# Splitting the attention scores around one projection group in steps 33 to 45 of a two-layer cross-attention kernel

## The chip, the cores and the metric

The kernel runs on one core of a Trainium2 chip. Its time is device microseconds (us) of that core, the median of three runs. The engines are TensorE (PE, with its weight loads shown apart as PEld), VectorE (DVE), ScalarE (ACT), GpSimd (POOL) and SyncE (SP), which here only issues DMAs. Each of them works through its own instructions in the order written, and they wait for each other by counting semaphores.

## The reference

There are 32 sequences of 64 tokens with 128 features, a context of the same shape, and a key mask. They pass a decoder layer (self-attention, cross-attention, feed-forward) and then a second cross-attention with rotary positions. The kernel treats this as three attention layers of 16 heads with 64 channels each; the change lies in the third:

```python
q = rope((x @ Wq).reshape(B, Sq, 16, 64)) / sqrt(64)      # x: output of the first layer
k = rope((ctx @ Wk).reshape(B, Skv, 16, 64))
v = (ctx @ Wv).reshape(B, Skv, 16, 64)
scores = einsum('bhqd,bhkd->bhqk', q, k)
attn = softmax(where(mask, scores, -1e9))
out = einsum('bhqk,bhkd->bqhd', attn, v).reshape(B, Sq, 1024) @ Wo
y = layernorm(x + out)
```

All of it is float32; a projection is three matmuls, on inputs and weights split into a high and a low part (L524 to L526).

## The kernel before

**Units and steps.** Two sequences (128 tokens) make a unit. 16 units times 3 attention layers are 48 pieces of work, numbered 0 to 47; a software pipeline of steps -2 to 49 overlaps them. Unit 32 is the first of the third layer. In step u TensorE does the scores of unit u, the transposes of the probabilities of an earlier unit, the weighted values and the output projection of unit u-2, the values of unit u, and half of the projections for the two units that come next: queries in an even step, keys in an odd one. The feed-forward part of the second layer still runs in steps 33 and 35 (every odd step up to there).

**Scores.** `scores(u)` writes the mask of all heads into ps_a (four PSUM banks, L553, 8 matmuls) and adds the products of queries and keys (L561, 64 matmuls of 32-row tiles, which the trace shows as 128). It starts when the exponentials of the unit before have been read out of ps_a and when the rotated keys are there. One semaphore, `scored`, is raised once, by the last of them.

**Fills and the ring.** Everything else that TensorE writes goes through a ring of four PSUM banks, ps_p0 to ps_p3. A *fill* is the filling of one bank (for the weighted values two). `fills(u)` lists the fills of a step in order, with the engine that empties each; fill number n uses bank n mod 4 and first waits until fill n-4 has been emptied (`bank_free`). The names in the list are:

- PP: transposes of the probabilities of unit u-2 (L660), copied out by ScalarE (L771).
- Qr or Kr, 0 to 3 (here r0 to r3): one quarter of the queries or keys (6 matmuls, L524 to L526), multiplied with the rotary tables by VectorE (L924), added by GpSimd (L1178). The tables' products have two buffers.
- O, two fills: weighted values (L601), copied out by ScalarE (L759).
- V, two fills: values (L649 to L651), copied by ScalarE (L769).
- FT (L700), F1, F2 (L716): feed-forward; FT transposes its input, split into high (ScalarE L764) and low part (VectorE L914).
- Y: output projection (L694), added to the residual by VectorE (L947).
- T: transposes of the inputs of the next queries (L639), at the end of an odd step, split into a high part by ScalarE (L762) and a low part by VectorE (L911). Query group r0 of the next step reads both.

**The order on the other engines.** VectorE's own list (`vector_order`) for such a step is: late feed-forward pieces, the maximum over the scores (L997), FT, r0 to r3, half of the normalisation of the unit before (L1042), the sums (L1027), Y and its statistics, F2, T. ScalarE goes through the fills in the order of `fills(u)`, with the first eight exponentials (L805) ahead of O and the other eight ahead of V; eight heads are scaled (L821) after V or F1, ahead of T.

Of the kernel before, what the change touches and what calls it, by code (L numbers as in the profile page):

```python
# [13 lines left out]
B, S, E = 32, 64, 128  # L14
H, D = 16, 64
PAIRS = H // 2
UNITS = B // 2
# [15 lines left out]
def projected(u):  # L33
    g = u // 2 + 1
    return g if g < N // 2 else None


def ffn_chunk(u):
    g = (u - 5) // 2
    return g if u % 2 and UNITS // 2 <= g < UNITS else None  # L40


def attends(u):
    return 0 <= u < N


def turns(u):
    return 0 <= u - 1 < N


def finishes(u):
    return 0 <= u - 2 < N


def rotary(u):
    return projected(u) is not None and projected(u) * 2 // UNITS == 2
# [7 lines left out]
def heads_in_ring(u):  # L64

    return finishes(u) and u >= 2 * UNITS
# [18 lines left out]
def by_head(u):  # L85

    return attends(u) and rotary(u)


def defers(u):  # L90

    return by_head(u) and u > 2 * UNITS - 1


def turned_by(u):

    return "AA" if by_head(u) or u >= N - 2 else "DD"
# [17 lines left out]
def fills(u):  # L115

    heads = [("O", b, "D" if u >= N and b else "A") for b in range(2)] if heads_in_ring(u) else []
    turn_in = [("T", 0, "AD")] if u % 2 == 0 and UNITS <= 2 * (u // 2 + 1) and projected(u) is not None and not by_head(u) else []
    values = [("V", j, "A") for j in range(2)] if attends(u) else []
    probabilities = [("P", j, turned_by(u)[j]) for j in range(2)] if turns(u) and not defers(u) else []  # L120
    deferred = [("PP", j, "A") for j in range(2)] if defers(u - 1) else []
    result = [("Y", 0, "D")] if finishes(u) else []
    project = []
    if projected(u) is not None:
        name = "K" if u % 2 else "Q"
        for j in range(4):
            project.append((name + "r", j, "D") if rotary(u) else (name, j, ("AAAD" if u == FIRST else "ADAD" if u < 0 else "AAAA")[j]))
    next_in = [("T", 0, "AD")] if u % 2 and by_head(u + 1) else []
    if by_head(u):

        ffn = [("FT", 0, "AD")], [("F1", 0, "A"), ("F1", 1, "A")], [("F2", 0, "D")]
        into, inside, outof = ffn if ffn_chunk(u) is not None else ([], [], [])
        return deferred + into + project[:2] + heads + project[2:] + values + inside + result + outof + probabilities + next_in
    if ffn_chunk(u) is not None:
        return [("FT", 0, "AD")] + values + probabilities + [("F1", 0, "A"), ("F1", 1, "A")] + project + [("F2", 0, "D")] \
            + result + next_in
    if u == N - 2:

        return deferred + values + heads + probabilities + result
    if u % 2:  # L140
        return heads + values + probabilities + project + result
    return deferred + heads + turn_in + values + probabilities + project[:3] + result + project[3:]
# [128 lines left out]
def build(nc, a, out):  # L271
    ctx = ExitStack()
    with ctx:
        def sb(name, shape, dt=F32):
            return ctx.enter_context(nc.sbuf_tensor(name, shape, dt))
# [4 lines left out]
        def sem(name):  # L280
            return ctx.enter_context(nc.semaphore(name))
# [43 lines left out]
        qT = sb("qT", [128, 2, PAIRS, CT])  # L325
        kT = sb("kT", [128, 2, PAIRS, CT])
# [37 lines left out]
        ps_a = ctx.enter_context(nc.psum_tensor("ps_a", [128, 4, 512], F32))  # L364
# [25 lines left out]
        scored = sem("scored")  # L390
# [69 lines left out]
        def head_at(u):  # L460
            return [n for n, _, _ in fills(u)].index("O")
# [58 lines left out]
        def _(pe):  # L520
            mm = nc.tensor.matmul
# [6 lines left out]
            def scores(u):  # L528
                par, v, layer = u // 2 % 2, u % 2, u // UNITS

                if by_head(u - 1):
                    pe.wait_ge(exped, EXPED.before(u))
                elif SHIFTED.before(u):
                    pe.wait_ge(shifted, SHIFTED.before(u))

                if layer == 2:

                    pe.wait_ge(rotated, ROTATED.at(u - 1 - v, "Kr", 3, v))
                elif v == 0:
                    out_of_bank(u - 1, "K", 2)  # L540
                    out_of_bank(u - 1, "K", 3)
                if layer == 2:
                    if u == 2 * UNITS:
                        pe.wait_ge(setup_dve, FOLD)

                        pe.wait_ge(headed, HEADED.before(u))


                    for i in range(4):
                        for b in range(2):  # L550
                            of = slice(32 * i, 32 * i + 32)
                            m = mask[of, 1, u % UNITS, b:b + 1, :]
                            mm(ps_a[64 * b:64 * b + 64, i ^ b, 0:256], fold[of, :], m.broadcast_to([32, 4, S]),  # L553
                               start=True, stop=False, skip_group_check=True)
                    for quad in range(H // 4):
                        for half in range(2):
                            for i in range(4):
                                for b in range(2):
                                    t = (2 * v + b) * S
                                    of = slice(32 * i, 32 * i + 32)  # L560
                                    last = mm(ps_a[64 * b:64 * b + 64, i ^ b, 64 * quad:64 * quad + 64],  # L561
                                              qT[of, par, 2 * quad + half, t:t + S], kT[of, par, 2 * quad + half, t:t + S],
                                              start=False, stop=half == 1, skip_group_check=True)
                    last.then_inc(scored, 1)
                    return


                for h in range(2):
                    for b in range(2):
                        of = slice(64 * h, 64 * h + 64)  # L570
                        m = mask[of, 0 if layer == 0 else 1, u % UNITS, b:b + 1, :]
                        mm(ps_a[64 * b:64 * b + 64, h ^ b, :], eye_bf[of, of], m.broadcast_to([64, 8, S]),  # L572
                           start=True, stop=False, skip_group_check=True)
                for p in range(PAIRS):
                    for h in range(2):
                        for b in range(2):
                            t = (2 * v + b) * S
                            of = slice(64 * h, 64 * h + 64)
                            last = mm(ps_a[64 * b:64 * b + 64, h ^ b, 64 * p:64 * p + 64],  # L579
                                      qT[of, par, p, t:t + S], kT[of, par, p, t:t + S],  # L580
                                      start=False, stop=True, skip_group_check=True)
                last.then_inc(scored, 1)

            def weight_values(u):
                w, last = u - 2, None
# [24 lines left out]
            def out_of_bank(u, name, j):  # L610

                who = {(n, k): w for n, k, w in fills(u)}[name, j]
                if "A" in who:
                    pe.wait_ge(act_emptied, EMPTY_A.at(u, name, j))
                if "D" in who:
                    pe.wait_ge(dve_emptied, EMPTY_D.at(u, name, j))
# [103 lines left out]
            def bias_of_values():  # L720

                for layer in range(2):
                    pe.wait_ge(multiplied, MULTIPLIED * (layer + 1))
                    mm(ps_a[:, 2 + layer, 0:E], valid[:, 2, 0:1].broadcast_to([128, 128]), products(layer)[:, 0, :],
                       start=True, stop=True).then_inc(bvwo_done, 1)
# [8 lines left out]
            for u in range(FIRST, END):  # L734
                if u in (0, READY):
                    pe.wait_ge(setup_dve, MASKED if u else FIRST_MASKED)
                if attends(u) and u != N - 1:
                    scores(u)
                if u == 2:
                    pe.wait_ge(bvwo_read, 2)  # L740
                if finishes(u) and not heads_in_ring(u):
                    weight_values(u)
                for at, (name, j, _) in enumerate(fills(u)):
                    if (u, name, j) == (N - 2, "P", 0):
                        scores(N - 1)
                    if (name, j) == ("O", 0):
                        weight_values(u)
                    elif name != "O":
                        fill(u, at, name, j)
                if u == 1:  # L750
                    bias_of_values()

# [595 lines left out]
```

## Time and profile before

| | us |
|---|---|
| median of 3 runs | 519.58 (519.25 to 519.75) |
| the profiled execution | 519.46 |
| its span in the trace | 517.6 |
| PE busy | 500.0 (97%) |
| DVE busy | 433.2 (84%) |
| ACT busy | 361.2 (70%) |
| POOL busy | 312.6 (60%) |

The span runs from the first to the last instruction that the trace records; 1.86 us of the profiled execution lie around it. Busy times of PE are modelled from pipelined matmuls: consecutive matmuls overlap in the list, and the distance between two starts is the better measure of what one costs. Steps 33 to 45 lie between 348.2 and 488.5 us; the first mask matmul (L553) of each step marks its start.

### The profile page before, as it was taken

The page shows a single profiled execution, that of the slowest core. Times are in us where ns is not written, and L with a number is a line of the kernel's source. Part 1 is how long each engine was busy: PE and PEld are TensorE (multiplying, and loading weights), DVE is VectorE, ACT ScalarE, POOL GpSimd, SP SyncE. Part 2 cuts the span into 40 slices and gives each one's busy share as a digit, 9 for nine tenths or more (in the row PEclk, how much of TensorE's full clock was granted, in tenths as well). Part 3 has the DMA queues.
Part 4 walks back from the last instruction along what each step waited for, and adds up shares of the span by engine and source line. Part 5 has one row for each costly group of instructions (what it writes and reads, how often), then busy time and mean ns, then how long its engine had stood idle before and what let it go on. Part 6 is the DMA issues. An engine that isn't in the chain of part 4 may idle for free.

```text
span 517.6 us, 23719 instructions
## 1 busy us (share of the span) xinstructions
PE 500.0 (97%) x10308; PEld 465.1 (90%) x10308; DVE 433.2 (84%) x761; ACT 361.2 (70%) x987; POOL 312.6 (60%) x611
## 2 busy tenths in 40 slices
PE   8889999999999999999999999999999999999985
PEld 7789999999999999999999997889999999999975
DVE  4988999978899878877778788998988888889883
ACT  6575765765866756756567685778687887888761
POOL 2836445536438545434646337888777887888735
PEclk9999999999999999999999999999999999999999
DMA  8910000000022010000000000000000000000000
GB/s 241 357 62 15 3 11 14 3 13 13 3 48 79 3 44 3 3 3 1 4 1 3 3 3 1 3 3 3 4 8 10 15 8 10 8 14 8 10 9 22
DMA packets 10039, 13.80 MB, mean 27 GB/s; under 512 B 848, under 2 KB 7376, under 8 KB 9936
## 3 DMA queue, kind: packets, MB, share of 16 engines
q1 hardware_dynamic: 9936, 12.28, 7.6%
q8 instruction: 82, 1.34, 1.1%
q14 instruction: 21, 0.17, 0.1%
HBM read 11.23 MB, written 1.05 MB: 24 GB/s over the span
## 4 chain that ended last, share of the span: by engine, by line
PE 78%; ACT 13%; DVE 4%; issue 2%; POOL 1%; DMA 1%; POOLq 0%; SPq 0%; DVEq 0%
PE ps_p L694 13%; PE ps_p L524 8%; PE ps_p L526 7%; PE ps_p L525 7%; PE ps_p L660 7%; ACT kT L777 6%; PE ps_a L579 5%; PE ps_a L601 5%; PE ps_p L649 5%; PE ps_a L561 4%; PE ps_p L651 4%; PE ps_p L650 4%; PE ps_p L601 3%; PE ps_p L716 2%; ACT probs L815 2%; PE ps_a L572 2%
## 5 line engine op out<-in xcount | busy, mean ns | idle before, releaser
L1217 POOL TENSOR_TENSOR small<-mv,epsilon 128x1 f32<-128x1 f32 x48 | 9.6, 199 | 147.5 <-DVE mv L953 147.5
L694 PE MATMUL ps_p<-wo,headsT 128*128 128x128 f32 x768 | 93.9, 275 | 1.6 <-DVE headsT L932 0.9
L694 PEld LDWEIGHTS ps_p<-wo,headsT 128*128 128x128 f32 x768 | 90.4, 192 | 3.5 <-DVE turn L924 1.1
L769 ACT ACTIVATE vv<-ps_p 128x512 f32<-128x512 f32 x96 | 57.1, 616 | 49.4 <-PE ps_p L651 46.1
L924 DVE TENSOR_TENSOR turn<-ps_p,rope 128x1024 f32<-128x1024 f32 x64 | 76.1, 1221 | 11.8 <-PE ps_p L526 10.2
L524 PE MATMUL ps_p<-xT_hi,wq_hi 128*128 128x256 f32 x192 | 58.8, 306 | 0.6 <-DVE wq_lo L1053 0.5
L805 ACT ACTIVATE probs<-ps_a,top 128x64 f32<-128x64 f32 x256 | 56.0, 353 | 4.3 <-DVE top L997 3.4
L1027 DVE TENSOR_REDUCE total<-probs 128x16 f32<-128x1024 f32 x48 | 58.1, 1210 | 0.2
L777 ACT ACTIVATE qT<-ps_p,columns 128x256 f32<-128x256 f32 x126 | 49.4, 496 | 10.2 <-PE ps_p L526 10.2
L1001 DVE TENSOR_REDUCE top<-ps_a 128x8 f32<-128x512 f32 x64 | 41.0, 683 | 18.1 <-PE ps_a L579 17.9
L526 PE MATMUL ps_p<-xT_hi,wq_lo 128*128 128x256 f32 x192 | 54.3, 283 | 0.3 <-issue 0.3
L525 PE MATMUL ps_p<-xT_lo,wq_hi 128*128 128x256 f32 x192 | 54.3, 283 | 0.0
L660 PE MATMUL ps_p<-eye,probs 128*128 128x128 f32 x384 | 50.9, 275 | 1.1 <-DVE probs L1042 1.1
L660 PEld LDWEIGHTS ps_p<-eye,probs 128*128 128x128 f32 x384 | 43.5, 141 | 6.5 <-ACT vv L769 1.3
L1178 POOL TENSOR_TENSOR qT<-turn 128x512 f32<-128x512 f32 x32 | 43.7, 1387 | 7.7 <-DVE turn L924 7.7
L1178 POOL TENSOR_TENSOR kT<-turn 128x512 f32<-128x512 f32 (+1 forms) x40 | 45.5, 1162 | 4.4 <-DVE turn L924 4.4
L777 ACT ACTIVATE kT<-ps_p,columns 128x256 f32<-128x256 f32 x124 | 47.5, 522 | 0.8 <-PE ps_p L526 0.8
L1042 DVE TENSOR_TENSOR probs<-probs,rinv 128x512 f32<-128x512 f32 x62 | 42.3, 720 | 1.0
L930 DVE COPY probsT<-ps_p 128x512 f32<-128x512 f32 x58 | 37.2, 682 | 6.1 <-PE ps_p L660 6.0
L524 PE MATMUL ps_p<-cT_hi,wk_hi 128*128 128x256 f32 x128 | 38.6, 302 | 0.1
L524 PEld LDWEIGHTS ps_p<-xT_hi,wq_hi 128*128 128x128 f32 x192 | 37.1, 193 | 1.7 <-issue 0.7
L771 ACT ACTIVATE probsT<-ps_p 128x512 f32<-128x512 f32 x38 | 20.6, 596 | 25.7 <-PE ps_p L660 25.7
(145 smaller groups left out, 1396.8 us busy)
## 6 DMA issues: line engine op xcount, KB each, us to landing
out<-y_out SPq DMA_DIRECT2D x16, 64.0 KB, 1.5
raw<-in_x_turned SPq DMA_DIRECT2D x1, 768.0 KB, 9.9
across<-in_across SPq DMA_DIRECT2D x1, 704.0 KB, 7.3
raw<-in_ctx_turned SPq DMA_DIRECT2D x5, 128.0 KB, 2.3
wq_raw<-in_L_xattn_sa_wq SPq DMA_DIRECT2D x2, 256.0 KB, 3.8
wk_raw<-in_L_xattn_sa_wk SPq DMA_DIRECT2D x1, 512.0 KB, 5.1
wv_raw<-in_L_xattn_sa_wv SPq DMA_DIRECT2D x1, 512.0 KB, 7.3
wo<-in_L_xattn_sa_wo SPq DMA_DIRECT2D x1, 512.0 KB, 8.5
```

What stands on the lines that cost most here:

```text
L524: mm(dst, w[0], x[0], start=True, stop=False)
L525: mm(dst, w[0], x[1], start=False, stop=False)
L526: return mm(dst, w[1], x[0], start=False, stop=True)
L660: last = nc.tensor.transpose(bank[:, 128 * pp:128 * pp + 128], probs[:, unit % 2, at_head:at_head + 2, :].rearrange("q h k -> q (h k)"), e ...
L694: last = mm(bank[:, 0:E], headsT[:, p, :, :].rearrange("r b q -> r (b q)"), wo[:, layer % 2, p, :], start=(p == 0), stop=(p == PAIRS - 1))
L769: ins = nc.scalar.activation(vv[:, u % 2, j, :, :].rearrange("k p d -> k (p d)"), bank[:, :], ACT.Copy)
L777: ins = nc.scalar.activation(to[:, g % 2, p, :], bank[:, CT * k:CT * k + CT], ACT.Identity, bias=bias[:, g * CU // UNITS, p:p + 1])
L805: ins = nc.scalar.activation(probs[:, u % 2, n, :], ps_a[:, bank, 64 * k:64 * k + 64], ACT.Exp, bias=top[:, at:at + 1], scale=scale)
L924: ins = V.tensor_tensor(turn[:, j % 2, :, :].rearrange("d a (h b t) -> d a h b t", h=2, t=S), bank[:, None, :].broadcast_to([128, 2, 512]) ...
L1027: V.tensor_reduce(total[:, :], probs[:, u % 2, :, :], AX_X, ALU.add).then_inc(dve_step, 1)
L1042: V.tensor_tensor(p, p, factor[:, u % 2, 8 * j:8 * j + 8, None].broadcast_to([128, 8, S]), ALU.mult)\
L1178: G.tensor_tensor(to[:, projected(u) % 2, 2 * j:2 * j + 2, of], *[t[:, :, of] for t in turned(j)], ALU.add).then_inc(rotated, 1)
```

## The change

In steps 33 to 45 TensorE's work is put in another order. `scores` now issues the masks and the first two of the four groups of score matmuls; then comes the first projection group r0 (in steps 33 and 35 the fill FT ahead of it), then the other two groups of score matmuls with the signal `scored`, and then the fills PP, r1, O, r2, r3 and so on. Before, the order was scores, PP, (FT,) r0, r1, O, r2, r3. Which matmuls there are does not change, nor does VectorE's list. ScalarE's list has FT ahead of PP in steps 33 and 35. Since the fills stand in another order, they sit in other banks of the ring.

```diff
+def scores_apart(u):
+
+    return by_head(u) and u > 2 * UNITS
...
-        return deferred + into + project[:2] + heads + project[2:] + values + inside + result + outof + probabilities + next_in
+        first, project = (project[:1], project[1:]) if scores_apart(u) else ([], project)
+        k = 2 - len(first)
+        return into + first + deferred + project[:k] + heads + project[k:] + values + inside + result + outof + probabilities + next_in
...
-                    for quad in range(H // 4):
...
-                    last.then_inc(scored, 1)
+                    score_quads(u, range(2))
+                    if not scores_apart(u):
+                        score_quads(u, range(2, 4))
                     return
...
+            def score_quads(u, quads):
+
+                par, v = u // 2 % 2, u % 2
+                for quad in quads:
+                    for half in range(2):
+                        for i in range(4):
+                            for b in range(2):
+                                t = (2 * v + b) * S
+                                of = slice(32 * i, 32 * i + 32)
+                                last = mm(ps_a[64 * b:64 * b + 64, i ^ b, 64 * quad:64 * quad + 64],
+                                          qT[of, par, 2 * quad + half, t:t + S], kT[of, par, 2 * quad + half, t:t + S],
+                                          start=False, stop=half == 1, skip_group_check=True)
+                if quad == H // 4 - 1:
+                    last.then_inc(scored, 1)
...
+                    if name[1:] == "r" and j == 0 and scores_apart(u):
+                        score_quads(u, range(2, 4))
```

TensorE's rows from the start of step 36 to its first projection group or second score half, before the change (ps_p0 to ps_p3 are the ring's banks, and brackets name the semaphores that a row waits for):

```order
L553 MATMUL ps_a<-mask,fold 64x256 [waits rotated,exped]
L553 MATMUL ps_a<-mask,fold 64x256 x7
L561 MATMUL ps_a<-kT,qT 64x64 x64
L660 MATMUL ps_p2<-eye,probs 128x128 [waits normed,act_emptied]
L660 MATMUL ps_p2<-eye,probs 128x128 x3
L660 MATMUL ps_p3<-eye,probs 128x128 [waits normed_rest,dve_emptied]
L660 MATMUL ps_p3<-eye,probs 128x128 x3
L524 MATMUL ps_p0<-xT_hi,wq_hi 128x256 [waits dve_emptied,act_emptied]
L525 MATMUL ps_p0<-xT_lo,wq_hi 128x256
L526 MATMUL ps_p0<-xT_hi,wq_lo 128x256
```

The same place of the changed kernel (its line numbers are other ones: L560 is the mask, L593 a score, L675 a transpose, L531 to L533 a projection):

```order
L560 MATMUL ps_a<-mask,fold 64x256 [waits rotated,exped]
L560 MATMUL ps_a<-mask,fold 64x256 x7
L593 MATMUL ps_a<-kT,qT 64x64 x32
L531 MATMUL ps_p2<-xT_hi,wq_hi 128x256 [waits dve_emptied,act_emptied]
L532 MATMUL ps_p2<-xT_lo,wq_hi 128x256
L533 MATMUL ps_p2<-xT_hi,wq_lo 128x256
L531 MATMUL ps_p2<-xT_hi,wq_hi 128x256
L532 MATMUL ps_p2<-xT_lo,wq_hi 128x256
L533 MATMUL ps_p2<-xT_hi,wq_lo 128x256
L593 MATMUL ps_a<-kT,qT 64x64 x32
L675 MATMUL ps_p3<-eye,probs 128x128 [waits normed,dve_emptied]
L675 MATMUL ps_p3<-eye,probs 128x128 x3
```

The r0 group has moved from behind eight transposes to the middle of the scores and from bank ps_p0 to ps_p2.

TensorE a little later in step 36, from the last r1 matmuls into O, before:

```order
L524 MATMUL ps_p1<-xT_hi,wq_hi 128x256
L525 MATMUL ps_p1<-xT_lo,wq_hi 128x256
L526 MATMUL ps_p1<-xT_hi,wq_lo 128x256
L601 MATMUL ps_p2<-probsT,vv 64x64 [waits act_emptied]
L601 MATMUL ps_p3<-probsT,vv 64x64
```

and in the changed kernel (L616 is O):

```order
L531 MATMUL ps_p1<-xT_hi,wq_hi 128x256
L532 MATMUL ps_p1<-xT_lo,wq_hi 128x256
L533 MATMUL ps_p1<-xT_hi,wq_lo 128x256
L616 MATMUL ps_p2<-probsT,vv 64x64 [waits dve_emptied,act_emptied]
L616 MATMUL ps_p3<-probsT,vv 64x64
```

O's first bank was last written by a PP fill before the change and is last written by r0 after it, and the first O matmul has gained a wait for VectorE.

## Rows read from the trace of the kernel before

**Rows 1.** The page: busy us, share of the span, instructions.
```profile
PE 500.0 (97%) x10308; PEld 465.1 (90%) x10308; DVE 433.2 (84%) x761; ACT 361.2 (70%) x987; POOL 312.6 (60%) x611
```

**Rows 2.** Windows, step 37 and a gap: length, busy (instructions), PEclk, DMA share, GB/s.
```profile
397.17:407.42 10.25, 10.25 (x257) 9.55 (x256) 9.35 (x14) 8.52 (x32) 8.38 (x13) 1.00 0.04 10
...
495.20:496.70 1.50, 0.01 (x2) 0.01 (x2) 0.27 (x2) 0.65 (x2) 0.00 (x0) 1.00 0.00 0
```

**Rows 3.** Timeline, step 37: start, length, engine, line, instruction, count [idle before].
```profile
397.17 0.32 PE L553 MATMUL ps_a<-mask,fold 32*64 32x256 bf16 x8
...
398.77 1.09 PE L660 MATMUL ps_p<-eye,probs 128*128 128x128 f32 x8
...
399.07 1.22 DVE L997 TENSOR_REDUCE top<-ps_a 128x16 f32<-128x1024 f32 x1
...
399.62 0.37 PE L524 MATMUL ps_p<-cT_hi,wk_hi 128*128 128x256 f32 x1
...
399.83 0.28 PE L525 MATMUL ps_p<-cT_lo,wk_hi 128*128 128x256 f32 x1
...
400.43 0.28 PE L524 MATMUL ps_p<-cT_hi,wk_hi 128*128 128x256 f32 x1
...
400.70 2.35 DVE L924 TENSOR_TENSOR turn<-ps_p,rope 128x1024 f32<-128x1024 f32 x2 [0.42 <-PE ps_p L526]
...
401.03 0.28 PE L526 MATMUL ps_p<-cT_hi,wk_lo 128*128 128x256 f32 x1
401.24 1.16 PE L601 MATMUL ps_p<-probsT,vv 64*64 64x64 f32 x64
```

**Rows 4.** Timeline, from the exponentials of step 37 to O of step 38.
```profile
403.43 1.75 ACT L805 ACTIVATE probs<-ps_a,top 128x64 f32<-128x64 f32 x8
...
407.42 0.32 PE L553 MATMUL ps_a<-mask,fold 32*64 32x256 bf16 x8
...
407.93 0.38 ACT L762 ACTIVATE xT_hi<-ps_p 128x256 fp32r<-128x256 f32 x1
...
408.60 0.39 DVE L911 TENSOR_TENSOR xT_lo<-ps_p,xT_hi 128x256 fp32r<-128x256 f32 x1
...
409.14 1.22 DVE L997 TENSOR_REDUCE top<-ps_a 128x16 f32<-128x1024 f32 x1 [0.15 <-PE ps_a L561]
...
411.49 1.16 PE L601 MATMUL ps_p<-probsT,vv 64*64 64x64 f32 x64
```

**Rows 5.** Timeline, step 33, with the feed-forward fill FT.
```profile
348.23 0.32 PE L553 MATMUL ps_a<-mask,fold 32*64 32x256 bf16 x8
...
350.76 0.38 PE L700 MATMUL ps_p<-eye,x 128*128 128x128 f32 x2
...
350.90 0.37 PE L524 MATMUL ps_p<-cT_hi,wk_hi 128*128 128x256 f32 x1
...
351.92 0.42 DVE L914 TENSOR_TENSOR x2T_lo<-ps_p,x2T_hi 128x256 fp32r<-128x256 f32 x1 [0.76 <-ACT x2T_hi L764]
...
352.26 2.34 DVE L924 TENSOR_TENSOR turn<-ps_p,rope 128x1024 f32<-128x1024 f32 x2
...
352.51 1.16 PE L601 MATMUL ps_p<-probsT,vv 64*64 64x64 f32 x64
...
354.66 0.39 PE L524 MATMUL ps_p<-cT_hi,wk_hi 128*128 128x256 f32 x1
```

**Rows 6.** Timeline, step 34.
```profile
362.15 0.32 PE L553 MATMUL ps_a<-mask,fold 32*64 32x256 bf16 x8
...
362.67 0.42 DVE L911 TENSOR_TENSOR xT_lo<-ps_p,xT_hi 128x256 fp32r<-128x256 f32 x1 [0.21 <-ACT xT_hi L762]
...
365.38 0.39 PE L526 MATMUL ps_p<-xT_hi,wq_lo 128*128 128x256 f32 x1 [0.29 <-issue]
...
366.78 1.16 PE L601 MATMUL ps_p<-probsT,vv 64*64 64x64 f32 x64
```

**Rows 7.** Timeline, a projection matmul near the kernel's start.
```profile
6.50 0.42 PE L525 MATMUL ps_p<-xT_lo,wq_hi 128*128 128x256 f32 x1
```

More of the change, by code:

```diff
@@ L554, in scores @@
                                start=True, stop=False, skip_group_check=True)
-                    for quad in range(H // 4):
[L556 to L563, printed above, removed]
-                    last.then_inc(scored, 1)
+                    score_quads(u, range(2))
+                    if not scores_apart(u):
+                        score_quads(u, range(2, 4))
                     return
```

## The prediction, made before the changed kernel ran

> **What bounds the kernel now.** I read the page's busy line first, then the windows, then the timeline of single steps. TensorE is busy for 500.0 of 517.6 us [rows 1], and in step 37 for 10.25 of 10.25 us at granted clock 1.00 [rows 2]: there is no idle time of TensorE in which a new wait could hide. VectorE and ScalarE have 0.9 and 1.7 us to spare in that step [rows 2]. So whatever holds TensorE up inside a step goes onto the end, and whatever only moves work about on the others does not, unless TensorE comes to wait for it. The question for each edit is which wait TensorE meets, and when it is released.
>
> I measure inside a step from its first mask matmul, t0, and need where O starts, because from O on nothing changes its order: the next step starts 407.42 - 401.24 = 6.18 us after O in step 37 [rows 3, 4], and the exponentials, copies, rotations and sums behind it follow from O and the r2 that comes after it. O starts at +4.07 in step 37 (401.24 - 397.17) and in step 38 (411.49 - 407.42) [rows 3, 4].
>
> **The change part by part.**
>
> *r0 ahead of the signal `scored`.* Masks and scores take 398.77 - 397.17 = 1.60 us [rows 3]. The masks are at most 0.32 of it, and as their ends overlap with the scores I take 0.24; a half of the scores is then 0.68 us. A projection group takes 400.43 - 399.62 = 0.81 us, where five spaces of 0.12 (400.43 - 399.83) and a first one of 0.21 show that changing the kind of matmul costs 0.09; from the last projection matmul to O it is 0.21 again (401.03 to 401.24), another 0.09 [rows 3]. The group in the middle therefore delays `scored` by 0.81 + 0.09 = 0.90 us. This switch was not between these two kinds in the trace; the bounds are 0 and 0.2 each, and I take 0.09, the value of both neighbours.
>
> *VectorE behind it.* VectorE's list is unchanged: maximum first, then r0. Where VectorE was free, the maximum started at +1.72 (409.14 - 407.42) [rows 4]; in step 37 it was late by itself, at +1.90 [rows 3], which the new delay covers. Now it starts at 1.72 + 0.90 = +2.62 and ends at +3.84 (1.22 long). r0's rotation follows at once, and takes 2.35 / 2 = 1.18 [rows 3]: it ends at +5.04. Before, it waited 0.42 us for its matmuls after the maximum [rows 3]; that idle time is gone, and it is the only thing won.
>
> *The bank that O wants.* With four banks in a ring, O's first fill is the fourth after r0 in the new order (r0, PP, PP, r1, O), so it waits for r0's rotation. Before, it followed a PP fill, emptied by ScalarE well in time. TensorE would be ready for O at +4.25 (4.07 and the two added switches), but the bank is free at +5.04. In step 33 the matmul that waited for a rotation (r3, 354.66) began 0.06 us after that rotation ended (352.26 + 2.34 = 354.60) [rows 5]. So O starts at 5.04 + 0.06 = +5.10, where it was +4.07: 1.03 us lost in each step, the switches included. r1's rotation follows r0's and is over at +6.2; r2's can come only after O (about 1.1 us) and r2's matmuls (0.81), at +7.0 or later, so the two buffers of the tables' products and GpSimd behind them are not late. Behind TensorE's waiting instruction stand r2, r3, V, Y and the next scores, the whole rest of the step. The exponentials' second half ended 403.43 + 1.75 = 405.18, 3.94 us after O [rows 3, 4], and the next scores come 6.18 after it, so this older wait keeps 2.2 us of slack.
>
> *r0 in an even step needs T.* Query group r0 reads the inputs that T turned at the end of the odd step before. Before the change r0 came at about +2.45, and the low part was ready at 408.60 + 0.39 - 407.42 = +1.57 [rows 4]. Now r0 is wanted at 0.24 + 0.68 = +0.92. T's split comes at the same distance from the step's start as before, because ScalarE reaches it behind work that hangs on O (407.93) and VectorE behind the statistics of Y (408.60). So r0 starts at 1.57 + 0.06 = +1.63, which is 0.71 us late, all of it ahead of `scored`: maximum at +3.3, r0's rotation done at +5.73, O at +5.79 or 0.7 more than in an odd step: 1.72 us lost in steps 38, 40, 42 and 44. In steps 34 and 36, behind a feed-forward step, the split was ready at 362.67 + 0.42 - 362.15 = +0.94 [rows 6], so r0 is 0.09 late there and the loss is 1.1 us.
>
> *Steps 33 and 35, with FT.* FT takes 350.90 - 350.76 = 0.14 of TensorE, also ahead of `scored` now. VectorE: maximum from 1.72 + 0.90 + 0.14 = +2.76 to +3.98, FT's low part to +4.3 (0.34 from 351.92 to 352.26), rotation of r0 to +5.5, O at +5.55; before it was 352.51 - 348.23 = +4.28 [rows 5]. r1 now waits for FT's bank, but that ends sooner than r0's rotation. Against the 1.27 stands the wait of r3 for the rotation of r1 that goes: from O at 352.51, with 1.1 for O and 0.8 for r2, it should have started at about 354.4 and did at 354.66, 0.2 late [rows 5]. I take 0.2 in both steps, so about 1.07 each.
>
> *The gap in step 34.* TensorE stood still for nothing that the trace names at 365.38, before O, and O came at +4.63 (366.78 - 362.15) instead of about +4.1 [rows 6]. Such a pause belongs to a place in the instruction stream; the new order puts the transposes there, which have 0.8 us of slack before O. So step 34 loses only 5.19 - 4.63, some 0.6 us. If the gap falls ahead of `scored` instead, 0.5 more.
>
> *Sum:* steps 37, 39, 41, 43, 45: 5 x 1.03 = 5.15. Steps 38, 40, 42, 44: 4 x 1.72 = 6.88. Steps 33 and 35: 2.15. Steps 34 and 36: 0.6 + 1.1 = 1.7. Together 15.9 us, against the profiled execution's own 519.46 (span 517.6 and 1.86 around it): 535.3. The median of the runs is 0.12 higher, so 535.5 us. Nothing after step 45 takes it back: step 46 starts from O of step 45 like any other. With both switches at 0 the sum is 2.3 less (13 x 0.18), with 0.2 each 2.9 more.
>
> **A rule weighed.** TensorE will stand still for 0.8 us in the middle of every step, and in every second step for 0.7 us more. In the trace a pause of 1.5 us in the scores of unit 47 (495.2 to 496.7, TensorE busy for 0.01) left the granted clock at 1.00, the 2.4 GHz level [rows 2].
>
> The Trainium skill says otherwise for a pattern like this: "TensorE: Matmul & The Clock Gate", section "A second HAM failure mode: psum-queue depth-cycling", tells of a kernel that cycled through PSUM banks, paused a little between groups of matmuls, and had its clock swing between the two levels. By the trace the term is 0; by that rule the time would be that of the rival on the clock below. The trace of before has no such regular pauses, so it neither agrees nor disagrees.
>
> **The rivals.**
>
> *T does not bind (the smaller loss).* If T's split is done by +0.9, every step loses the 1.03 to 1.1 of the bank wait alone: 15.9 - 4 x 0.69 = 13.1, or 532.7 us. Against it: ScalarE's copy starts at +0.51 and ends at +0.89 in step 38, and VectorE only takes the low part up at +1.18 [rows 4]; what stands ahead of both hangs on O.
>
> *A second chain turns late (the larger loss).* ScalarE's exponentials follow the maximum, the copies of O follow them, and the second exponentials follow those; then V and the scaling. If one of these comes to hold the next scores, 0.3 to 0.6 us more per step, 4 to 8 us: 539 to 543. Against it: 2.2 us of slack as worked out above.
>
> *The clock falls.* At the lower level a projection matmul took 0.42 us at the kernel's start against 0.28 [rows 7, 3], with the work of a step near double. If the clock were low for a fifth of the 13 steps, that is some 2.5 x 10 = 25 us more: 560.
>
> *Not slower: the bank is free in time.* VectorE waits 0.42 us for r0's matmuls today [rows 3], so whoever takes VectorE for the late engine sees it gain: r0 is there when the maximum ends, r3's waits in steps 33 and 35 vanish, and TensorE pays nothing as long as r0's rotation ends by +4.25 in a step. Then the time is 519.2 (519.6 less 0.4). The deciding point is that rotation: by my sum it ends at +5.04. It would have to start before the maximum, or maximum and rotation would have to be 0.8 us shorter together than their rows. The list has the maximum first, so I give it little.
>
> **How the numbers follow.** Forecast as summed 0.73, T not binding 0.12, a second chain 0.07, the clock 0.03, not slower 0.05. The forecast's own spread comes from the switches (-2.3, +2.9) and the gaps (0.5): 533.2 to 538.9. The range of 531.5 to 540 takes in the case in which T does not bind and the near end of the larger loss. Under 0.2% (1.0 us) nothing can be told from no change. All but the last case are slower, 0.95; of its 0.05 I put 0.03 on the same and 0.02 on faster.
>
> **What would show it.** In the profile after: TensorE idle before O (L616), released by VectorE's rotation, about 0.8 us in each of 13 steps; idle before the first projection matmul of even steps from 38 on, released by VectorE's xT_lo, about 0.7 us; the rotation right behind the maximum with no idle time; steps 37 to 45 of 11.3 us where odd (5.10 + 6.18) and 11.8 where even (no T at the end). The chain of waits should show L924 and L997 with a share each. It is wrong if O starts before +4.5, if the mask of the next step comes later than 6.3 us after O, or if the granted clock leaves 1.00.

## The result, and the profile after

The changed kernel takes 540.02 us (median of 5 runs, 539.03 to 541.28) against 519.59 us before (5 runs): slower, ratio 1.039, 95% interval 1.0371 to 1.041. The forecast was 535.5 us with a range of 531.5 to 540: the direction and the mechanism held, the size was 4.5 us short, and the median stands at the upper end of the range. The profiled execution took 541.28 us and its span is 539.4 us.

The page of the changed kernel, first part, answers to [rows 1]:

```profile
PE 506.7 (94%) x10308; PEld 469.0 (87%) x10308; DVE 431.6 (80%) x761; ACT 360.4 (67%) x987; POOL 311.3 (58%) x611
```

The same instructions, but TensorE stands still for 32.7 us of the span where it did for 17.6. What it waited for is in the view of waits, for TensorE from 345 to 520 us (waiting line, releaser: us in total, times, longest):

```profile
PE ps_p L616 <- DVE turn L941: 10.5, 13, 0.9
PE ps_p L531 <- DVE xT_lo L928: 2.9, 4, 0.7
PE ps_a L593 <- issue: 1.6, 1, 1.6
PE ps_p L531 <- ACT probsT L788: 1.4, 2, 0.7
```

Thirteen waits of O (L616) for the rotation, four of the first projection matmul for T's low part: the counts are those of the forecast. The third row is the pause in unit 47's scores, which the kernel before had too [rows 2]. The fourth is named wrongly, as shown below.

Windows after (length, busy (instructions) of PE, PEld, DVE, ACT, POOL, PEclk, DMA share, GB/s): from the first mask matmul of step 33 to that of step 46, step 37, step 38, from unit 47's scores to the end, and a piece of that:

```profile
348.86:508.66 159.80, 144.74 (x3375) 132.23 (x3375) 121.20 (x172) 113.76 (x408) 112.11 (x161) 1.00 0.03 8
402.31:413.89 11.58, 10.68 (x259) 9.74 (x258) 9.37 (x14) 8.52 (x32) 8.36 (x13) 1.00 0.03 9
413.89:426.01 12.12, 10.48 (x256) 9.55 (x256) 8.73 (x13) 8.34 (x31) 8.01 (x12) 1.00 0.03 8
...
513.76:539.40 25.64, 18.85 (x429) 17.37 (x422) 13.68 (x28) 9.78 (x18) 9.94 (x23) 0.92 0.06 16
518.12:521.53 3.41, 3.41 (x18) 3.33 (x16) 1.76 (x3) 2.08 (x4) 0.00 (x0) 0.50 0.03 5
```

The first and fourth stretch before the change:

```profile
348.23:488.48 140.25, 139.63 (x3375) 130.02 (x3375) 122.74 (x172) 114.16 (x408) 112.28 (x161) 1.00 0.03 9
...
493.56:517.50 23.94, 17.22 (x429) 15.79 (x422) 13.72 (x28) 9.78 (x18) 9.96 (x23) 0.96 0.06 17
```

So 159.80 - 140.25 = 19.55 us lie in the thirteen changed steps. Of the 21.8 us between the two profiled executions, 0.6 lie ahead of step 33, where no instruction is changed, and 1.6 behind the start of step 46, where TensorE ran for 3.41 us at half the clock (last row). By what is on record it does not depend on the change: the traces of e2, e3 and e6 have such a stretch too (e3 a second one, at about 17 to 23 us), those of before, e1, e4, e5, e7, e8 and e10 do not, though e4 and e7 make TensorE wait at O as this kernel does. Executions of either kernel with a mean clock of 0.995 or 0.996 are the longer ones: 541.2 and 541.3 us against 539.0 to 540.0 for the changed kernel, and in the rounds of e1 to e4 520.8 to 521.3 against 518.8 to 519.7 for the kernel before. Below, experiments are compared by the time from step 33's to step 46's first mask matmul, called *the stretch*, 140.25 us before and 159.80 after.

The timeline of step 37 after, answering to [rows 3] (start, length, engine, line, instruction [idle before]):

```profile
402.31 0.32 PE L560 MATMUL ps_a<-mask,fold 32*64 32x256 bf16 x8
...
403.27 0.40 PE L531 MATMUL ps_p<-cT_hi,wk_hi 128*128 128x256 f32 x1
...
403.98 0.28 PE L533 MATMUL ps_p<-cT_hi,wk_lo 128*128 128x256 f32 x1
...
404.19 0.92 PE L593 MATMUL ps_a<-kT,qT 32*64 32x64 f32 x64
...
405.03 1.09 PE L675 MATMUL ps_p<-eye,probs 128*128 128x128 f32 x8
405.14 1.23 DVE L1014 TENSOR_REDUCE top<-ps_a 128x16 f32<-128x1024 f32 x1 [0.79 <-PE ps_a L593]
...
406.28 2.35 DVE L941 TENSOR_TENSOR turn<-ps_p,rope 128x1024 f32<-128x1024 f32 x2
...
407.58 2.53 POOL L1195 TENSOR_TENSOR kT<-turn 128x512 f32<-128x512 f32 x2 [0.64 <-DVE turn L941]
...
407.76 1.16 PE L616 MATMUL ps_p<-probsT,vv 64*64 64x64 f32 x64 [0.90 <-DVE turn L941]
```

The reader is to see the chain: r0's last matmul ends at 404.26, but VectorE stands idle for 0.79 us, because its next instruction is the maximum and the scores end at 405.0. The rotation follows at 406.28, and O starts at 407.76, 5.45 us after the step's start where it was 4.07.

Step 38, answering to [rows 4]:

```profile
414.40 0.41 ACT L779 ACTIVATE xT_hi<-ps_p 128x256 fp32r<-128x256 f32 x1
...
415.12 0.39 DVE L928 TENSOR_TENSOR xT_lo<-ps_p,xT_hi 128x256 fp32r<-128x256 f32 x1
415.65 0.36 PE L531 MATMUL ps_p<-xT_hi,wq_hi 128*128 128x256 f32 x1 [0.74 <-DVE xT_lo L928]
...
420.11 1.10 PE L616 MATMUL ps_p<-probsT,vv 64*64 64x64 f32 x60 [0.90 <-DVE turn L941]
```

r0 waits for T's low part and starts 1.76 us into the step (415.65 - 413.89) instead of 0.96, and O comes at 6.22.

Step 33, answering to [rows 5]:

```profile
353.00 0.41 DVE L931 TENSOR_TENSOR x2T_lo<-ps_p,x2T_hi 128x256 fp32r<-128x256 f32 x1
353.34 2.52 DVE L941 TENSOR_TENSOR turn<-ps_p,rope 128x1024 f32<-128x1024 f32 x2
...
353.57 0.36 PE L531 MATMUL ps_p<-cT_hi,wk_hi 128*128 128x256 f32 x1 [0.72 <-ACT probsT L788]
...
354.81 1.16 PE L616 MATMUL ps_p<-probsT,vv 64*64 64x64 f32 x64 [0.28 <-DVE turn L941]
```

r1 wants FT's bank, which VectorE empties at 353.41, and starts 0.16 later. The profile puts this wait down to ScalarE's probsT, which r1 has nothing to do with; the program's order tells who it is (r1's bank is FT's). It shortens the wait at O to 0.28.

### The profile page after: what moved, and what is told of

It is laid out like the page before. It is cut to its first block, busy times and chain, and to the rows that moved or that the text cites. A ratio compares the mean times of both kernels' runs of the same rounds, so it can differ in the third digit from the quotient of the medians.

```text
span 539.4 us, 23721 instructions
## 1 busy us (share of the span) xinstructions
PE 506.7 (94%) x10308; PEld 469.0 (87%) x10308; DVE 431.6 (80%) x761; ACT 360.4 (67%) x987; POOL 311.3 (58%) x611
## 4 chain that ended last, share of the span: by engine, by line
PE 69%; ACT 12%; DVE 10%; issue 5%; POOL 1%; DMA 1%; SPq 0%; POOLq 0%; DVEq 0%
PE ps_p L709 12%; PE ps_p L531 7%; ACT kT L794 6%; PE ps_p L532 6%; PE ps_p L533 6%; PE ps_a L579 5%; PE ps_a L616 5%; DVE turn L941 5%; PE ps_a L593 4%; PE ps_p L664 4%; PE ps_p L675 4%; PE ps_p L616 4%; PE ps_p L666 3%; PE ps_p L665 3%; PE ps_p L731 2%
## 5 line engine op out<-in xcount | busy, mean ns | idle before, releaser
L709 PE MATMUL ps_p<-wo,headsT 128*128 128x128 f32 x768 | 95.5, 278 | 1.6 <-DVE headsT L949 0.9
L709 PEld LDWEIGHTS ps_p<-wo,headsT 128*128 128x128 f32 x768 | 92.0, 194 | 3.5 <-DVE turn L941 1.1
L531 PE MATMUL ps_p<-xT_hi,wq_hi 128*128 128x256 f32 x192 | 59.1, 308 | 3.1 <-DVE xT_lo L928 2.9
L794 ACT ACTIVATE qT<-ps_p,columns 128x256 f32<-128x256 f32 x126 | 49.3, 496 | 10.2 <-PE ps_p L533 10.2
L533 PE MATMUL ps_p<-xT_hi,wq_lo 128*128 128x256 f32 x192 | 54.1, 282 | 0.0
L675 PE MATMUL ps_p<-eye,probs 128*128 128x128 f32 x384 | 50.9, 275 | 1.0 <-DVE probs L1059 1.0
L675 PEld LDWEIGHTS ps_p<-eye,probs 128*128 128x128 f32 x384 | 43.5, 141 | 6.3 <-ACT vv L786 1.2
L531 PEld LDWEIGHTS ps_p<-xT_hi,wq_hi 128*128 128x128 f32 x192 | 37.0, 193 | 4.8 <-ACT xT_hi L779 3.4
L531 PE MATMUL ps_p<-cT_hi,wk_hi 128*128 128x256 f32 x128 | 38.8, 303 | 1.4 <-ACT probsT L788 1.4
```

The costliest lines, as they stand in the source:

```text
L531: mm(dst, w[0], x[0], start=True, stop=False)
L533: return mm(dst, w[1], x[0], start=False, stop=True)
L675: last = nc.tensor.transpose(bank[:, 128 * pp:128 * pp + 128], probs[:, unit % 2, at_head:at_head + 2, :].rearrange("q h k -> q (h k)"), e ...
L709: last = mm(bank[:, 0:E], headsT[:, p, :, :].rearrange("r b q -> r (b q)"), wo[:, layer % 2, p, :], start=(p == 0), stop=(p == PAIRS - 1))
L794: ins = nc.scalar.activation(to[:, g % 2, p, :], bank[:, CT * k:CT * k + CT], ACT.Identity, bias=bias[:, g * CU // UNITS, p:p + 1])
```

## The experiments

The theory: TensorE's waits for VectorE (O for r0's rotation behind the maximum, r0 for T) make most of the loss. The rivals: the cut itself does (TensorE's own time), or later chains do. Diffs are against the changed kernel unless said otherwise; ratios are to the kernel before in the same rounds.

**e1: r0's rotation (and FT) ahead of the maximum on VectorE.**

```diff
-        return fout + fgain + maxima + those("FT") + those("Qr", "Kr") + before ...
+        early, rest = (those("FT") + those("Qr", "Kr")[:1], those("Qr", "Kr")[1:]) if scores_apart(u) else ...
+        return fout + fgain + early + maxima + rest + before ...
```

> The changed kernel (540.0 us), but in steps 33 to 45 VectorE takes FT and the rotation of r0 ahead of the maximum over the scores. Theory A (O waits for r0's rotation, which waits behind the maximum): the wait before O is gone; what stays is 0.40 us per step of TensorE's own (measured in the trace after: the scores end 2.72 us after the step's start with r0's 0.72 in them, where 1.60 + 0.72 would do) and the wait for T in steps 38, 40, 42, 44 (0.81 each): 519.6 + 13 x 0.40 + 4 x 0.81 less the 1.1 of pauses and r3 waits that the change removed = about 527 us. Theory B (TensorE pays for the split itself and for the changes of the kind of matmul; the order on VectorE is only seen in passing): 538 to 540 us. Theory C (the later maximum holds the exponentials and through them the next scores): slower than 540.

Measured: 528.4 us (ratio 1.0164, 1.0139 to 1.019); the stretch is 148.66, 11.1 us shorter than after the change. Step 37 of e1 begins at 398.02:

```profile
400.08 1.23 DVE L942 TENSOR_TENSOR turn<-ps_p,rope 128x1024 f32<-128x1024 f32 x1
...
401.22 1.21 DVE L1015 TENSOR_REDUCE top<-ps_a 128x16 f32<-128x1024 f32 x1
401.44 1.09 ACT L789 ACTIVATE probsT<-ps_p 128x512 f32<-128x512 f32 x2 [2.17 <-PE ps_p L676]
...
402.62 1.16 PE L617 MATMUL ps_p<-probsT,vv 64*64 64x64 f32 x64
```

All that TensorE waited for in e1 from 345 to 515 us:

```profile
PE ps_p L532 <- DVE xT_lo L929: 3.4, 4, 0.9
PE ps_a L594 <- issue: 2.1, 1, 2.1
```

The wait at O is gone, O comes at +4.60. That is 0.13 later than the 4.07 and the cut's 0.40, some 1.7 us in thirteen steps, and so most of what e1 is above the 527 expected. By the rows, ScalarE's second copy of PP (401.44 + 1.09 = 402.53) is now the last thing O needs; no run tested that alone. The wait for T has stayed. Theory A holds, C falls, and B keeps the 0.40 per step only.

**e2: the change in odd steps alone.**

```diff
-    return by_head(u) and u > 2 * UNITS
+    return by_head(u) and u > 2 * UNITS and u % 2 == 1
```

> The change in the seven odd steps 33 to 45 alone. If each step's loss is its own (5 x 1.32, 2 x 1.34 by the trace after) and the wait for T belongs to even steps that issue r0 early: 519.6 + 9.3 = 529 us, with even steps back at 10.04 us from start to start. Rival: losses pass from one step to the next (an even step pays for the odd step before it), then even steps stay longer than 10.04 and the time is 531 to 535.

Measured: 528.3 us (ratio 1.017, 1.0141 to 1.0199), the stretch 148.59. Two mask matmuls and the O between them:

```profile
399.41 0.32 PE L560 MATMUL ps_a<-mask,fold 32*64 32x256 bf16 x8
...
404.85 1.16 PE L616 MATMUL ps_p<-probsT,vv 64*64 64x64 f32 x64 [0.91 <-DVE turn L941]
...
410.98 0.32 PE L560 MATMUL ps_a<-mask,fold 32*64 32x256 bf16 x8
```

Step 37 takes 11.57 us, as after the change (11.58), and step 38 takes 10.03, as before it (10.04). Each step pays for itself, and no wait for T is left in the trace. The odd steps' losses are those of the changed kernel, 9.3 us in seven steps; the stretch grew by only 8.34, because the pauses that the kernel before has in steps 34 and 36 are gone here. By the table below, the six even steps have the larger share of the 19.55, 10.2 us.

**e3: half the maximum.**

```diff
+                    kept = S // 2 if scores_apart(u) else S
-                                    ps_a[:, :, 0:256].rearrange("q m (f k) -> q m f k", k=S), AX_X, ALU.max,
+                                    ps_a[:, :, 0:256].rearrange("q m (f k) -> q m f k", k=S)[:, :, :, 0:kept], AX_X, ALU.max,
```

> The changed kernel, with VectorE's maximum in steps 33 to 45 taken over the first 32 of each head's 64 keys (the softmax is shifted by another number than the maximum). The instruction is about 0.54 us shorter (1024 elements against 512: 1.22 against 0.68 us in the trace). Theory A: each of the 13 steps is shorter by just that, 540 - 7 = 533 us, and the idle time before O falls from 0.9 to about 0.4. Theory B: no change, 540 us.

Measured: 534.2 us (ratio 1.0278, 1.0238 to 1.0317), the stretch 152.81, 6.99 us shorter for an expected 7. Step 37, which begins at 402.17:

```profile
405.00 0.69 DVE L1015 TENSOR_REDUCE top<-ps_a 128x16 f32<-128x512 f32 x1 [0.81 <-PE ps_a L593]
405.61 2.43 DVE L941 TENSOR_TENSOR turn<-ps_p,rope 128x1024 f32<-128x1024 f32 x2
...
407.08 1.11 PE L616 MATMUL ps_p<-probsT,vv 64*64 64x64 f32 x61 [0.37 <-DVE turn L941]
```

The maximum is 0.54 us shorter and O 0.54 us earlier (+4.91 against +5.45), one for one. The maximum is on the path in each of the thirteen steps. The median is only 5.9 us below that of the changed kernel, because three of e3's four runs have a mean clock of 0.989 to 0.995; the fourth, at 0.999, took 532.2 us against 539.0 and 539.1.

**e4: two waits ahead of O instead of four.**

```diff
-                for j in range(2):
-                    ...
-                        bank_free(u, head_at(u) + b)
+                if scores_apart(u):
+                    pe.wait_ge(act_emptied, EMPTY_A.at(u, "PP", 1))
+                    pe.wait_ge(dve_emptied, EMPTY_D.at(u, "Qr" if u % 2 == 0 else "Kr", 0))
+                else: ...
```

> The changed kernel, with the waits ahead of O's first matmul put down as two (one for ScalarE's last copy, then the one for VectorE) instead of four with VectorE's third. In the trace after, O starts 0.25 us after the end of r0's rotation where r3 in step 33 of before, with one wait, started 0.06 after. If the order and number of waits make that: 13 x 0.15 to 0.2 less, 537.5 to 538 us, and O at +5.3 instead of +5.45. If the delay belongs to how TensorE restarts after standing still, no change.

Measured: 537.7 us (ratio 1.0344, 1.0315 to 1.0373), the stretch 158.40, 1.4 us shorter. Step 37 begins at 401.48:

```profile
405.45 2.34 DVE L945 TENSOR_TENSOR turn<-ps_p,rope 128x1024 f32<-128x1024 f32 x2
...
406.81 1.16 PE L620 MATMUL ps_p<-probsT,vv 64*64 64x64 f32 x64 [0.79 <-DVE turn L945]
```

O now starts 1.36 us after the rotation does, where it was 1.48 (407.76 - 406.28): about 0.11 saved (0.79 us of waiting for 0.90), half of what was in question. The edit changed the number and the order of the waits at once, so which of the two counts is open. Of the rest, some 0.14 after the rotation's end, the same is seen at r0 in step 38 (415.65, 0.14 after 415.51). Why one wait in step 33 of before was met within 0.06 [rows 5] stays open.

**e7: T ahead of the values in steps 37, 39, 41, 43.**

```diff
-        ... project[k:] + values + inside + result + outof + probabilities + next_in
+        turned, next_in = (next_in, []) if scores_apart(u) and ffn_chunk(u) is None else ([], next_in)
+        ... project[k:] + turned + values + inside + result + outof + probabilities + next_in
```

(and T's low part right behind the rotations in VectorE's list)

> The changed kernel, but in steps 37, 39, 41 and 43 the fill T comes ahead of the values (V) on TensorE, and its copies ahead of V on ScalarE and of the normalisation on VectorE. Theory A (in steps 38, 40, 42, 44 r0 waits 0.81 us for T's low part): r0 at +0.96 instead of +1.77 there, even steps 11.3 us instead of 12.13; against that up to 0.2 us in the odd steps where Y's bank now was r3's. 537 us. Rival: r0 waits for something else there (its bank, or the rotation tables' buffer): 540 us and r0 still at +1.77.

Measured: 538.3 us (ratio 1.0376, 1.0357 to 1.0396), the stretch 158.48. The end of step 37 and the start of step 38:

```profile
412.15 0.41 DVE L930 TENSOR_TENSOR xT_lo<-ps_p,xT_hi 128x256 fp32r<-128x256 f32 x1
412.29 2.05 PE L711 MATMUL ps_p<-wo,headsT 128*128 128x128 f32 x16 [0.17 <-DVE turn L943]
414.27 0.32 PE L562 MATMUL ps_a<-mask,fold 32*64 32x256 bf16 x8
...
415.23 0.39 PE L533 MATMUL ps_p<-xT_hi,wq_hi 128*128 128x256 f32 x1
```

T's low part is ready before the step starts, r0 comes at +0.96, and the even steps take 11.35 instead of 12.13 us. The odd ones give 0.45 of that back (12.03 against 11.58), more than the 0.2 expected: Y now waits for r3's rotation (0.17 in the row); the other 0.28 came with T's new place behind r3, and what makes them was not tested. T was what r0 waited for; the repair is worth less than half of it, and the time is 538.3 us where 537 was expected.

**e5: the cut around PP instead of around r0.** The fills stand as in the kernel before, and the second half of the scores follows the second PP fill.

```diff
-        return into + first + deferred + project[:k] + heads + project[k:] + ...
+        return deferred + into + project[:2] + heads + project[2:] + ...
-                    if name[1:] == "r" and j == 0 and scores_apart(u):
+                    if (name, j) == ("PP", 1) and scores_apart(u):
```

> The scores come in two halves in steps 33 to 45, but around the two PP fills instead of around r0; all fills stand in the order and banks of the kernel before, so O does not wait for a rotation and r0 does not come before T is ready. Theory A (waits made the loss, the split itself costs TensorE 0.40 us per step as seen in the traces after and e1): about 519.6 + 13 x 0.40, less or more by the pauses for instructions in steps 34 and 36: 524 to 525 us, O at +4.47. Theory B (any split is as costly as this one): 535 or more.

Measured: 525.1 us (ratio 1.0123, 1.0097 to 1.015), the stretch 145.79. Step 37 of e5:

```profile
398.40 0.32 PE L558 MATMUL ps_a<-mask,fold 32*64 32x256 bf16 x8
...
400.39 0.91 PE L591 MATMUL ps_a<-kT,qT 32*64 32x64 f32 x64
...
401.23 0.39 PE L529 MATMUL ps_p<-cT_hi,wk_hi 128*128 128x256 f32 x1
...
402.87 1.16 PE L614 MATMUL ps_p<-probsT,vv 64*64 64x64 f32 x64
```

O comes at +4.47 with no wait in front of it: a cut costs TensorE 0.40 us in itself. The second half of the scores takes 0.84 us (400.39 to 401.23), the same as around r0. The rest of the step takes 0.14 more; r3 starts 0.2 us after the matmul before it (404.88 against 404.68) instead of 0.12, behind a rotation of r1 that is later too. That explains at most a part of the 0.14; the rest is open.

**e6: r0 ahead of the masks, scores uncut, odd steps alone** (diff against e2).

```diff
-                    score_quads(u, range(2))
-                    if not scores_apart(u):
-                        score_quads(u, range(2, 4))
+                    score_quads(u, range(4))
-                if attends(u) and u != N - 1:
+                if attends(u) and u != N - 1 and not scores_apart(u):
                     scores(u)
-                        score_quads(u, range(2, 4))
+                        scores(u)
```

> In the seven odd steps r0 (with FT where there is one) comes ahead of the masks and of all scores, which are not split; even steps as in the kernel before. Against e2 (the change in odd steps alone, 528.3 us, O at +5.44) only the cut through the scores is gone. If the cut costs 0.2 us (insertion of r0 measured 1.12 us where the group and its two switches should take 0.90), O comes at +5.2 and the time is 526.8 us. If the 0.2 belong to something else, such as r0 in front of the scores as a whole, 528 us as e2.

Measured: 527.6 us (ratio 1.0159, 1.0136 to 1.0182). From r0's first matmul, step 37:

```profile
398.99 0.37 PE L531 MATMUL ps_p<-cT_hi,wk_hi 128*128 128x256 f32 x1
...
399.88 0.32 PE L560 MATMUL ps_a<-mask,fold 32*64 32x256 bf16 x8
...
401.49 1.09 PE L673 MATMUL ps_p<-eye,probs 128*128 128x128 f32 x8
...
404.21 1.16 PE L614 MATMUL ps_p<-probsT,vv 64*64 64x64 f32 x64 [0.91 <-DVE turn L939]
```

Masks and scores take their old 1.61 us (399.88 to 401.49). From r0 of step 37 to r0 of step 39 it is 21.21 us (398.99 to 420.20), against 21.60 for the same pair of steps in e2. So the uncut order saves 0.39 per odd step, twice what was expected: 0.22 of it ahead of O, which comes 5.22 us after the step's first matmul instead of 5.44, and 0.17 at the seam, where r0 follows the output projection directly. r0 ahead of the scores costs its bare 0.72, and everything above that is the cut. O still waits 0.91 for the rotation, since the maximum stays ahead of it. The median gained only 0.7 us on e2, where 7 x 0.39 would be 2.7; pauses with no releaser take a part of it, such as some 0.4 us in step 36 of e6, where e2 has none, and the rest is open.

**e8: e1 and e7 together.**

> Both e1 (VectorE takes r0's rotation ahead of the maximum) and e7 (T ahead of the values). Against e1 (528.4 us) the wait for T goes, 0.9 us in each of four steps, and up to 0.2 us come back at Y in four steps: 525 to 525.5 us. What is left over 519.6 is then the split itself (0.40) and 0.13 us in which O waits for ScalarE's copy of PP. If waits were not what made these steps longer, 528 us. If the kernel came out at or below 519.6, the split itself would be worth having, which I do not expect.

Measured: 526.7 us (ratio 1.0156, 1.0134 to 1.0178), the stretch 146.96. All that TensorE waited for from 345 to 495 us:

```profile
PE ps_p L712 <- DVE turn L944: 0.7, 4, 0.2
```

With both waits gone, 6.7 of the 19.55 us are left. O comes 0.53 later than before in each of the nine steps from 37 on (the cut's 0.40 and the 0.13 of e1) and 1.15 in all in steps 33 to 36, where the kernel before had its pauses; behind O, T's new place costs 0.41 in four steps, and the other steps are 0.9 shorter together. It is still slower than the kernel before; the cut has nothing to win where TensorE never stood still.

**e10: the kernel before with one wait ahead of O.**

```diff
+                if by_head(u) and defers(u - 1) and ffn_chunk(u) is None:
+                    pe.wait_ge(act_emptied, EMPTY_A.at(u, "PP", 1))
+                else: ...
```

> The kernel before, with one wait ahead of O's first matmul in steps 34 and 36 to 45 instead of four, all for ScalarE and all long met when TensorE arrives. In e4 fewer waits ahead of O brought 0.11 us per step, where the wait was really met late. If waits cost TensorE time whether they are met or not, O comes at +3.97 instead of +4.07 and the kernel gains 1.1 us (518.5). If only a late release pays for the waits behind it, no change: 519.6 and O at +4.07.

Measured: 520.1 us (ratio 1.0014, 0.9998 to 1.0031), O at +4.08 in step 37 (401.56, the step from 397.48). No change: waits that are met already cost TensorE nothing that can be seen here. No version that beats the kernel before was found.

## Why the prediction was right, and where it was short

| steps | lost, forecast | lost, measured | from start to start, before and after |
|---|---|---|---|
| 37, 39, 41, 43 | 1.03 each | 1.32 | 10.26, 11.58 |
| 45 | 1.03 | 1.38 | 10.14, 11.52 |
| 38, 40, 42, 44 | 1.72 each | 2.09 | 10.04, 12.13 |
| 33, 35 | 1.07 each | 1.35 | 13.92, 15.27 |
| 34 | 0.6 | 0.85 | 10.61, 11.46 |
| 36 | 1.1 | 0.97 | 10.49, 11.46 |
| all | 15.9 | 19.55 | 140.25, 159.80 |

**What bounds.** Right. The instructions' busy time did not grow beyond the cut's cost, and each wait of TensorE went onto the end, local to its step (e2).

**The bank wait.** Right in place, number and cause (e1, e3). The size was 0.3 short in each step, from two terms of the sum that were put too low. First, r0 in the middle of the scores was put at 0.90 us; it is 1.12 (405.03 - 402.31 = 2.72 against 1.60 [rows 3]). I priced two changes of kind at 0.09 each, from neighbours where one kind ends for good. The cut costs 0.40, by e5, and by e6 it is the cut and not the moved group; that is the upper bound stated for the two changes together, and not the value taken. That the second half of the scores takes 0.84 us (404.19 to 405.03) where 0.68 was assumed shows in the trace; what in the array makes it so was not tested. Second, O was to start 0.06 us after the rotation and starts 0.26 after (407.76 against 406.28 + 1.22); 0.11 of that goes with the four waits ahead of O (e4). The maximum and the rotation together were 0.05 shorter than I had them. The rest of the step after O was 6.18 in the forecast and is 6.13.

**T in even steps.** Right (e7, and e2 where it vanishes); r0 was expected at +1.63 and came at +1.76: T's low part was ready at +1.62 instead of +1.57, and r0 started 0.14 after it instead of 0.06. (The recorded sum has the rotation done at +5.73, where 5.04 + 0.71 is 5.75.)

**Steps 33 and 35.** The sum took r1's wait for FT's bank as harmless. It was the longer one (0.72 us, O only 0.28 more), though what it delays is caught up in the same wait: O at +5.95 against +5.55 forecast, by the same two terms; FT, put at 0.14, moved r0 by 0.19 (+1.15 against +0.96).

**The pauses.** The pause of step 34 indeed no longer counted. The kernel before has one in step 36 too (O at +4.52), which the forecast overlooked when it took +4.07 there; it vanished as well, so that O came only 1.03 us later than before. The close agreement in step 36 (1.1 and 0.97) is luck: the 0.45 overlooked is nearly cancelled by O coming at +5.55 where +5.19 was forecast. The forecast also held that a pause belongs to a place in the instruction stream. One does: that of unit 47's scores, 1.4 to 2.1 us, is in all eleven traces. But in e10, whose instruction stream hardly differs from the kernel before, the small ones sit elsewhere (none in step 34, O at +4.81 in step 36). Only sums over many steps should be read.

**The rivals.** T not binding: falls, its wait is in the trace. A second chain turning late: falls; the next scores kept their distance from O, in e1 ScalarE's copies bound by 0.13 only. Not slower: falls on the point named; the rotation ended at 5.2 us, not by 4.25. The clock: in the thirteen steps, with 14.8 us of regular pauses, the granted clock is 1.00 (the window row above). The Trainium skill ("TensorE: Matmul & The Clock Gate", section "A second HAM failure mode: psum-queue depth-cycling") tells of a kernel whose clock swung between its levels under frequent short idles between groups of matmuls; for pauses of up to 0.9 us twice in 12 us, this trace does not show it. The forecast priced the lower level from a matmul at the kernel's start [rows 7]; the granted clock of that stretch (6.50 to 6.92 us) is 1.00 in the record, so that row does not show what the lower level costs. The tail of the changed kernel does: sixteen matmuls of the output projection (L709) take 3.51 us from their first to the start of O there (518.13 to 521.64, granted clock 0.50), where the same sixteen of the kernel before (L694) take 1.88 (497.92 to 499.80, granted clock 1.00).

## What to carry to other kernels

Before an instruction is moved in a kernel whose buffers form a short ring, count who comes one ring length behind it: here O inherited a bank whose reader stood behind the maximum on VectorE, and that wait, not the work, was more than half of the loss (11.1 of 19.55 us by e1). Then ask what the moved piece itself reads and when that used to be ready: r0 moved forward by 1.5 us overtook its own input. And where the busiest engine never stands still, there was nothing for a cut of its work to win here, and each one cost 0.40 us; the price of a cut is best taken from a cut, not from a place where one kind of work simply ends.

## What the runs showed of the hardware that was not expected

- A run of 128 small score matmuls (32-row tiles), cut in two by six full-size matmuls, costs TensorE 0.40 us in all; six full-size matmuls ahead of the run cost only their 0.72 us. Around eight transposes (e5) the cut costs the same 0.40.
- When TensorE has to wait for VectorE at an instruction with four waits, it starts 0.26 us after VectorE's end; with two waits and the late one last, 0.14. Waits that are met already cost nothing that can be seen (e10).
- TensorE standing still for 0.74 to 0.9 us once or twice in each of thirteen steps left the granted clock at 1.00. Yet a stretch of some 3.4 us at 0.50 came near the end in four of eleven traces (after, e2, e3, e6). In all four it begins behind the 1.5 to 1.6 us pause in unit 47's scores; the other seven have a pause of 1.4 to 2.1 us there too, and behind it their granted clock is still 1.00. What decides it is open.
